# Raw weights in two waves, banded scores by pairs, and relu-shared maxima for three more tiles in a one-core transformer kernel

## What is computed

```python
x = x + attn_a(layernorm(x))        # x: (2, 1024, 128) f32; 16 heads of 8; full softmax
x = x + ffn(layernorm(x))           # 64 experts, top 6 of 4 of 8 groups, and a shared expert
x = x + attn_b(layernorm(x))        # the same with a mask: key j counts for query i if i-31 <= j <= i
x = x + ffn(layernorm(x))           # the same weights as in the first ffn

def attn(x):                        # biases on q, k, v and the output
    scores = einsum('bhqd,bhkd->bhqk', Q, K) / sqrt(8)
    return softmax(scores) @ V @ Wo + bo
```

## Time and profile before

| | us |
|---|---|
| median of 3 runs | 1168.04 (1163.45 to 1170.56) |
| profiled execution, its own time | 1164.44 |
| its span, first to last instruction | 1162.6 |
| busy: PE, DVE, ACT, POOL | 1046.3, 927.4, 706.3, 461.6 |
| mean granted TensorE clock | 0.937 |

### The profile page before, as it was taken

How to read it: one execution, slowest core, us unless ns; L and a number is a source line. 1 busy time by engine, 2 the same in 40 slices (tenths; PEclk the granted TensorE clock), 3 DMA queues, 4 the chain that set the end, 5 groups by cost and what they waited for, 6 DMA issues and landing times. The chain is left out here.

```text
span 1162.6 us, 18837 instructions
## 1 busy us (share of the span) xinstructions
PE 1046.3 (90%) x6308; PEld 425.8 (37%) x6308; DVE 927.4 (80%) x2139; ACT 706.3 (61%) x1083; POOL 461.6 (40%) x434
## 2 busy tenths in 40 slices
PE   5669999999999979999999996777888999999997
PEld 4212222222222325444445442333434544444443
DVE  8588999999998467889788776765775879877775
ACT  2445878777777765666656663444455566666664
POOL 4116246433100105565554553100112566555554
PEclk8657999999999989999999998688979999999999
DMA  8411303311200126666765981122205667687662
GB/s 306 112 36 29 79 2 78 79 45 35 54 2 1 42 74 162 164 175 175 194 164 150 223 195 40 51 70 74 74 3 143 159 153 187 173 196 202 186 186 57
DMA packets 72185, 131.63 MB, mean 113 GB/s; under 512 B 12680, under 2 KB 47624, under 8 KB 72088
## 3 DMA queue, kind: packets, MB, share of 16 engines
q1 hardware_dynamic: 69600, 122.50, 40.9%
q10 hardware_dynamic: 2488, 7.93, 1.9%
HBM read 115.08 MB, written 14.91 MB: 112 GB/s over the span
## 5 line engine op out<-in xcount | busy, mean ns | idle before, releaser
L419 ACT ACTIVATE Aatt_prob<-Aatt_st 128x1024 f32<-128x1024 f32 x256 | 247.7, 1022 | 73.3 <-PE Aatt_st L314 72.3
L485 DVE TENSOR_REDUCE Aatt_mx<-Aatt_sc 128x1 f32<-128x512 f32 x451 | 280.6, 683 | 12.0 <-PE Aatt_sc L301 11.5
L1980 POOL TENSOR_TENSOR M1ex_low<-M1ex_hid,M1ex_high 128x512 f16<-128x512 f32 x132 | 152.7, 1157 | 135.9 <-ACT M1ex_high L1879 68.4
L1980 POOL TENSOR_TENSOR M2ex_low<-M2ex_hid,M2ex_high 128x512 f16<-128x512 f32 x132 | 152.7, 1157 | 129.6 <-PE M2ex_acc L1835 72.1
L301 PE MATMUL Aatt_sc<-ks,qs 48*128 48x512 bf16 x496 | 152.9, 408 | 33.9 <-DMA ks<-stack 11.2
L1873 ACT ACTIVATE M2ex_sil<-M2ex_ring,unscale 128x512 f32<-128x512 f32 x132 | 90.7, 687 | 92.4 <-PE M2ex_ring L1818 92.1
L1873 ACT ACTIVATE M1ex_sil<-M1ex_ring,unscale 128x512 f32<-128x512 f32 x132 | 90.7, 687 | 90.2 <-PE M1ex_ring L1818 89.7
L325 PE MATMUL Aatt_pv<-Aatt_prob,vg 128*32 128x512 f32 x1024 | 138.5, 613 | 0.6 <-ACT Aatt_prob L419 0.6
L1917 DVE SCALAR_TENSOR_TENSOR M2ex_ring<-M2ex_ring,unscale,M2ex_sil 128x512 f32<-128x512 f32 x132 | 100.0, 758 | 39.9 <-ACT M2ex_sil L1873 39.3
L1917 DVE SCALAR_TENSOR_TENSOR M1ex_ring<-M1ex_ring,unscale,M1ex_sil 128x512 f32<-128x512 f32 x132 | 99.9, 757 | 37.0 <-ACT M1ex_sil L1873 33.7
L301 PEld LDWEIGHTS Aatt_sc<-ks,qs 48*128 48x128 bf16 x496 | 35.9, 93 | 206.3 <-DVE Aatt_mx L485 171.4
(11 more groups left out here) (433 smaller groups left out, 1922.8 us busy)
## 6 DMA issues: line engine op xcount, KB each, us to landing
M1ex_cb<-comb SPq DMA_DIRECT2D x130, 256.0 KB, 4.1
M2ex_cb<-comb SPq DMA_DIRECT2D x130, 256.0 KB, 4.1
M_wt<-wsplit SPq DMA_DIRECT2D x132, 192.0 KB, 4.0
wsplit<-split_cut SPq DMA_DIRECT2D x9, 704.0 KB, 4.5
qs<-stack SPq DMA_DIRECT2D x32, 96.0 KB
ks<-stack SPq DMA_DIRECT2D x30, 96.0 KB
split_raw<-in_wg_dram ACTq DMA_DIRECT2D x3, 704.0 KB, 8.3
split_raw<-in_wu_dram ACTq DMA_DIRECT2D x3, 704.0 KB, 13.2
```

The costliest lines, as they stand in the source:

```text
L419: act.activation(prob[e % 4][:, :, :].rearrange("p a c -> p (a c)"), st[pr][:, :, :].rearrange("p a c -> p (a c)"), ACT.Exp, scale=SCALE). ...
L485: ins = dve.tensor_reduce(mx[k][:, m, h:h + 1], scores, AX.X, ALU.max)
L1980: pool.tensor_tensor(low[q % 3][:, :], hid[q % 3][:, :], high[q % 3][:, :], ALU.subtract).then_inc(low_ready, 1)
```

## The change

Six edits, all in the order of work:

1. `split_load` takes a wave. Wave 0 (the three pieces of wg) is issued where all nine were; wave 1 (six pieces) is issued by ACT behind its half of group 0's load.
2. In `start` the loads of group 0 wait for the two stores of group 0 alone (`first_stored`), and no more for all eight of the batch.
3. The maximum of piece 3 leaves the end of `start`; it is now taken with the other five behind group 0's maxima in `attend_full`.
4. Tiles 1 to 3 of group 1, in front of the loop, are shared with ACT as group 0's are. Group 0's turned maxima go to the bank `pv` and no longer to a bank of the scores.
5. In the banded attention `scores` does one half (both its heads, `h`), and the loop issues half 0 in front of the transposed scores and half 1 behind them. In front of the loop the halves follow one another too.
6. The banded attention's eight stores of batch 1 move from SP, where they stood behind `max_rows` of group 2, to ACT's `second_batch`, one per slice.

```diff
@@ attend_full
-            if n == 0:
-                return (0, 1) if blk else ()
+            if n < 2:
+                return (0, 1) if 0 < blk < STEPS and (n == 0 or blk < AHEAD) else ()
...
         def turn_bank(n):
-            return sc[bank_index(n + 1, TURN_TILE)][:, :].bitcast(BF16)[0:3 * HG * TB, 0:P]
+            bank = sc[bank_index(n + 1, TURN_TILE)] if n else pv
+            return bank[:, :].bitcast(BF16)[0:3 * HG * TB, 0:P]
...
-                if i == TURN_TILE and n:
+                if i == TURN_TILE and n > 1:
                     pe.wait_ge(m_copied, n)
...
-            split_tops(dve, weights, 3)
+            split_tops(dve, weights, 2)
@@ attend_banded, SP
-                if n + 3 == G:
-                    store_stacks(sp, env, v2, 1)
@@ attend_banded, PE
-            def scores(n, k, qt):
+            def scores(n, k, qt, pr):
...
+                    blocks = score_blocks(s, k, nxt, nxt2)
+                    for off, kk, qt in blocks:
+                        scores(n + off, kk, qt, 0)
                     for h in range(2):
                         for pr in range(2):
...
                     next(beside, None)
-                    for off, kk, qt in score_blocks(s, k, nxt, nxt2):
-                        scores(n + off, kk, qt)
+                    for off, kk, qt in blocks:
+                        scores(n + off, kk, qt, 1)
@@ attend_banded, ACT
                 yield from qkv_scalar(act, env, v2, bank, 1)
+                for i in range(2):
+                    act.wait_ge(v2.low_ready, 2 * i + 2)
+                    act.wait_ge(v2.mid_ready, 2 * i + 2)
+                    for g in range(G):
+                        act.dma_start(env.stack[i, G + g].rearrange("s r t -> r s t"),
+                                      v2.part[32 * g:32 * g + 32, i, :, :]).then_inc(env.stored[1], 16)
+                        yield
@@ start, SP
-            store_stacks(sp, env, v, 0, (0,))
-            sp.wait_ge(env.stored[0], STORES)
+            store_stacks(sp, env, v, 0, (0,), first_stored)
+            sp.wait_ge(first_stored, 32)
             load_half_group(sp, 0)
+            sp.wait_ge(env.stored[0], STORES - 32)
@@ start, ACT
-            split_load(act, env.weights)
+            split_load(act, env.weights, 0)
...
-            store_stacks(act, env, v, 0, (1,))
+            store_stacks(act, env, v, 0, (1,), first_stored)
             act.wait_ge(keys_set, 2)
-            act.wait_ge(env.stored[0], STORES)
+            act.wait_ge(first_stored, 32)
             load_half_group(act, 1)
+            split_load(act, env.weights, 1)
@@ start, DVE
             rest_of(norm)
-            split_tops(dve, env.weights, 2)
@@ pieces
-TOPS = ((0, 1), (2,), (3,), (4, 5, 6, 7, 8))
+WAVES = ((0, 1, 2), (3, 4, 5, 6, 7, 8))
+TOPS = ((0, 1), (2,), (3, 4, 5, 6, 7, 8))
```

More of the change, by code:

```diff
@@ L323, in weigh @@
                     pe.wait_ge(u_out, ONE + n * 2 + qh)
+                    pe.wait_ge(m_copied, 1)
                 for j in range(HG):
@@ L351, in _ @@
                     if n == 1 and 4 * blk == TURN_TILE:
-                        turn_max(0, 0, True)
+                        turn_max(0, 0, False)
                     for part in range(4):
@@ L651, in _ @@
         def _(pe):
-            def scores(n, k, qt):
+            def scores(n, k, qt, pr):
                 first = 0 if qt else WIN
+                rows = slice(HALF * pr, HALF * pr + MAXROW)
+                pe.wait_ge(red_done, n * 2 * STEPS + 2 * qt + pr + 1)
                 for h in range(2):
-                    for pr in range(2):
-                        if h == 0:
-                            pe.wait_ge(red_done, n * 2 * STEPS + 2 * qt + pr + 1)
-                        rows = slice(HALF * pr, HALF * pr + MAXROW)
-                        mm = pe.matmul(sc[pr][:, h * BAND + first:(h + 1) * BAND], qs[k][rows, h, qt * P:(qt + 1) * P],
-                                       ks[k][rows, h, qt * P - WIN + first:(qt + 1) * P], start=True, stop=True)
-                        if h == 1:
-                            mm.then_inc(sc_done, 1)
+                    mm = pe.matmul(sc[pr][:, h * BAND + first:(h + 1) * BAND], qs[k][rows, h, qt * P:(qt + 1) * P],
+                                   ks[k][rows, h, qt * P - WIN + first:(qt + 1) * P], start=True, stop=True)
+                mm.then_inc(sc_done, 1)
             def weigh(n, k, s):
@@ L703, in _ @@
                 for qt in range(STEPS if n == 0 else AHEAD):
-                    scores(n, n, qt)
+                    for pr in range(2):
+                        scores(n, n, qt, pr)
                 if n == 0:
@@ L856, in start @@
         sem = lambda n: semaphore(nc, env, f"start_{n}")
-        x_in, x1_in, projections_in, loaded, made, ones_set, keys_set, biased = map(sem, (
-            "x_in", "x1_in", "projections_in", "loaded", "made", "ones_set", "keys_set", "biased"))
+        x_in, x1_in, projections_in, loaded, made, ones_set, keys_set, biased, first_stored = map(sem, (
+            "x_in", "x1_in", "projections_in", "loaded", "made", "ones_set", "keys_set", "biased", "first_stored"))
         bank = side_banks(nc, ctx, "start")
@@ L1046, in splitter, with split_load @@
     return w
-def split_load(sp, w):
-    for q, (i, j) in enumerate(PIECES):
+def split_load(sp, w, wave):
+    for q in WAVES[wave]:
+        i, j = PIECES[q]
         sp.dma_start(w.raw[q][:, :, :], w.sources[i][:, j:j + PIECE, :]).then_inc(w.raw_in[q], 16)
@@ L1649, in qkv_scalar, with store_stacks @@
     yield
-def store_stacks(sp, env, v, b, which=(0, 1)):
+def store_stacks(sp, env, v, b, which=(0, 1), first_stored=None):
     for i in which:
@@ L1658, in store_stacks @@
             sp.dma_start(env.stack[i, b * G + g].rearrange("s r t -> r s t"),
-                         v.part[32 * g:32 * g + 32, i, :, :]).then_inc(env.stored[b], 16)
+                         v.part[32 * g:32 * g + 32, i, :, :]).then_inc(
+                             first_stored if first_stored and g == 0 else env.stored[b], 16)
 def qkv_vector(dve, env, v, bank, b, lows=True):
```

## The result

The median after is 1149.61 us (1145.16 to 1156.67, four executions) against 1168.28 (1163.45 to 1170.56, four). The ratio is 0.9874, 95% interval 0.9845 to 0.9902, which is 0.0126 x 1165 = 14.7 us faster. The profiled execution of the changed kernel took 1145.16 us with a span of 1143.3 and a mean granted clock of 0.948. It is the shortest of its four, so the two spans differ by more (19.3 us) than the ratio says. Over its four executions the time goes with the clock: 1145.16 and 1147.8 at 0.948, 1151.42 at 0.944, 1156.67 at 0.936.

A forecast was written before the change was run, and what follows sets the result against it. No single engine bounds it (PE busy 90%); waits at start, before the banded loop and for group 4. Terms -7.2, +0.8, -4.0, -4.7, -0.8, +1.6, -1.0 sum to -15.3 us: 1149.1 profiled, median 1152.7, range 1142 to 1163.

The forecast's parts named there:

- Start: Start: group 0's loads issued at 26.0 instead of 33.9, PE's first score at 35.2, 7.2 us earlier.
- The second wave's rival: Start: the second wave takes the loads' DMA time, gain 3.5 us instead of 7.2, total 1156.4; chance 0.17.
- Behind group 0's maxima: First attention: sixth maximum delays the maxima's rows, PE waits for them, shared tiles save DVE time; +0.8 us.
- In front of the banded loop: Before the banded loop: half by half, PE fills one bank while DVE reads the other; -4.0 us.
- The wait for group 4: Banded loop: with stores on ACT, PE's wait for group 4's keys falls from 6.8 to 2.1 us; -4.7 us.
- the clock behind it: Banded loop, behind the stall for group 4: a shorter stall saves part of the low-clock loss; -0.8 us.
- ACT's stores: Banded loop: eight stores at 0.45 us each on ACT, four between a step's two exponentials; +1.6 us.
- The order in the banded loop: Banded loop: fewer PE and DVE waits, against half 0's matmuls delaying the transposed scores; -1.0 us.
- loop gains more: Banded loop: DVE's waits vanish in further steps, -6 us instead of -1.0, total 1147.7; chance 0.15.
- Pairs in turn lose the overlap: Banded loop: one half's matmuls in a row lose overlap, +10 us instead of -1, total 1163.7; chance 0.15.
- The slower rival: Banded loop: exponentials wait for DVE's reduction of the tile before, 0.6 us per step, total 1185; chance 0.04.

The follow-up runs named there:

- first_only: Kernel before, with group 0's loads waiting for group 0's two stores alone, all nine raw pieces still in front: 1164.42 us, ratio 0.9987.
- waves_only: Kernel before, with raw pieces in two waves and piece 3's maximum moved behind group 0, all eight stores still waited for: 1162.75 us, ratio 0.9982.
- shared_only: Kernel before, with tiles 1 to 3 of group 1 shared and group 0's turned maxima in bank `pv`: 1165.66 us, ratio 1.001.
- front_only: Kernel before, with scores half by half only in front of the banded loop, the loop in its old order: 1162.62 us, ratio 0.9969.
- act_stores_only: Kernel before, with only batch 1's eight stores moved to ACT: 1158.45 us, ratio 0.9946.
- stores_twice: Changed kernel, with each of ACT's eight stores issued a second time into a spare DRAM tensor: 1164.82 us, ratio 1.0004.
- old_loop: Changed kernel, with the banded loop's scores wholly in the old order, half by half only in front of it: 1150.62 us, ratio 0.9873.
- pairs_only: Kernel before, with scores half by half both in front of the banded loop and in it, nothing else: 1165.4 us, ratio 1.0009.
- five_first: Changed kernel, with five raw pieces in the first wave and maxima of pieces 2 and 3 taken where DVE waits: 1142.7 us, ratio 0.9812.

## Why the prediction was right, point by point

The median was forecast at 1152.7 us and came at 1149.6, 3.1 below, inside the range; the gain was forecast at 15.3 us and is 14.7 by the ratio. That it comes so close is in part luck: a term that was 2.4 us too small, the wait for group 4 with the stores, stands against a loop order that brought nothing and a start a little short, and one mechanism behind group 0's maxima was wrong at the right size. The terms, each against what it measured:

**Start, -7.2.** It was -6.55 (35.9 for 35.2). The chain was as foretold: landing 3.8 us against 3.3 assumed, loads at 25.8 against 26.0, but load issue to first score took 10.1 us against 8.5 + 0.7. One profile each cannot split this step: it took 9.3 us in first_only and 9.4 in waves_only, but between 8.3 and 9.4 in the five profiles with the start as before, and between 9.0 and 10.1 in the four with the change's. The means of the two groups, 8.8 and 9.5, differ by the 0.7 us of the estimate, and their first scores by 7.1 us, the size of the term. The second wave's rival asked for a first score near 39 and has fallen. first_only and waves_only show that the waves are the larger part and that the narrow wait adds to them.

**Behind group 0's maxima, +0.8.** It was +0.85 from the run of maxima on, but not for the reason given: I had PE wait for the rows. I added their landing to the end of the six issues, and it counts from the last issue: 84.2 + 1.8 = 86.0, while PE is busy with group 1's scores up to the first transposed one at 86.89. The tiles set that moment, before too (89.1 + 1.8 = 90.9, and 92.30). So +0.85 is the sixth maximum in full, +1.5 (waves_only, 17.7 for 16.2), less 0.6 for the shared tiles and the bank `pv` (shared_only, 15.6 for 16.2). A tile of group 1 took 2.21 us against my 2.0. Another 0.3 us went between the first score and the run, within chance.

**In front of the banded loop, -4.0.** It was -3.7 in the profile and -3.6 by front_only's ratio. The tile took 1.21 us against 1.25.

**The wait for group 4, -4.7, the clock behind it, -0.8, and ACT's stores, +1.6.** Together -3.9, and act_stores_only measured -6.3 (interval -8.2 to -4.3, from its ratio times 1165): the group was mis-sized. Two steps failed. I had the load go out at 778.4 and left 2.1 us of the wait. In act_stores_only, whose loop starts 2.3 us later than that of before, the last store was issued at 775.5, landed in 2.4 us and not 3.3, and the load went out at 778.0, by the time of before near 775.7. The buffer too was free some 2 us before my 777.3, with group 1's last transposed scores, which start at 775.05 in the trace of before. What bound the load was the last store, 0.6 us there and 0.7 in the change; 0.2 us of PE's wait stayed, in the change none. And a store's issue was counted in full between two exponentials, while it runs beside the one in front of it: spacing 0.33 to 0.41 us with a store between, 0.33 without, and group 1 of act_stores_only no longer than before. A second issue in a row costs more, on average up to 0.55 us (stores_twice).

**The order in the banded loop, -1.0.** It was about 0 (old_loop has the same ratio as the change, to within some 4 us by the intervals), and partly right in mechanism: less waiting for DVE, more for ACT. By groups at the full clock in both it is -0.7 in group 4 (21.5 for 22.2), -0.25 in group 6 and +0.8 in group 3. On the kernel before, the order lost some 4.7 us with the clock (pairs_only against front_only), which no term had. The rival "loop gains more" has fallen by old_loop: the 12.1 us that the loop gained in the profile are the wait (group 2) and the clock, not the order. Its number, 1147.7, came closer than the forecast's, for the wrong reason.

**Pairs in turn lose the overlap.** This rival asked for +10 from one half's matmuls standing next to each other. The rows at 727.24 speak against it: the Trainium skill (TensorEngine Tiling (Array Packing), Key Properties) says that different tiles "operate independently", and the trace agrees further than I took it. Here they run beside each other even when two or three matmuls lie between them in program order, and in old_loop, where the halves alternate, the time is the same: no loss of overlap shows. What I drew from the page, that the halves must alternate in the code, was mine and was wrong.

**The slower rival** asked for transposed scores that wait for DVE. All waits of PE's scores for DVE in the loop are 4.2 us, 6 times; it did not decide.

Summed, the measured parts (-6.55 + 1.14 to the first transposed score, -3.6, -6.3 and about 0 for the order) are -15.3 us, against -14.7 by the ratio; they mix times of single executions with ratios of medians, so an agreement to the microsecond is more than they can show. Not settled is what sets the clock. It is the largest thing that the prediction did not have: pairs_only, stores_twice and the first five_first had groups 0 and 4 at 22.7 and 27.4 us. In the profiled executions 27.4 stands only where half 0 is in front (three of five), and 22.6 or more in group 0 only where the stretch ahead is half by half (five of nine, with 21.2 once). That busier stretches ahead draw the low clock is no more than argued, and these counts are too few to call either a cause. The executions of pairs_only and front_only do show that on the kernel before half 0 in front goes with a lower clock; in the changed kernel it does not show (0.936 to 0.948 in its four executions, 0.940 to 0.952 in old_loop's six). Which execution gets which clock was not explained.

## What to carry to other kernels

When small stores stand in front of a critical load, count what else is in flight on the DMA engines: to split the bulk load in two waves halved the landing, and to narrow the wait paid only after that. When two things come late behind the same run of work, look in the trace which of them is there last before you name the bound: here the rows of maxima had landed 0.9 us before the tiles were through. A wait that names a transfer is to be followed back to the queue on which it was issued; eight issues that stood behind an unrelated wait cost 6 us. And a change in order that saves one engine's waits should be tried with its front and its loop apart: here the front was worth 3.6 us, and the loop nothing in the changed kernel and a loss on the kernel before.

## What the runs showed of the hardware

- Matmuls on the two halves of the rows (0 to 47 and 64 to 111) run beside each other here without standing side by side in the program: at 727.24 a score and a transposed score start, by the code's order the first and the fourth of the eight matmuls behind a step's masks, and the eight start in pairs 0.10 to 0.14 us apart.
- The same instructions took 21.5 or 27.4 us (group 4) and 14.8 or 19.5 (group 6) as the granted clock was 1.00 or 0.69 and 0.50. For one program (five_first) the executions lie at 1141.4 to 1143.0 with a mean clock of 0.949 to 0.950, and at 1152.9 with 0.934. For a kernel like this, four executions can be off by several us.
- An issue of a DMA on ACT (0.35 us) lay beside the exponential before it, and the next exponential came 0.33 to 0.41 us after that one, 0.33 without an issue. Second issues right behind the first took 0.46 to 1.21 us and cost on average at most 0.55.
- The 192 KB stores landed 7.8 to 8.6 us after their issue with nine raw pieces of 704 KB issued before them, 3.4 to 3.8 with three.
